# New tables of places for the work order of attention and tail in a hybrid block kernel

## The chip, the cores and the metric

The kernel runs on one core of one Trainium2 chip. The metric is the device time of one launch in microseconds.

## What is computed

The block takes x of shape (2, 1024, 256) in float32 and does four things, each added to x and each behind a layer norm:

- **Attention by a gated delta rule**, 16 heads of 128. Queries, keys and values are projections of the normed x, run through a causal convolution of four taps and a silu. A decay gate per channel and a factor beta per head go with them. For each time step: `S = S * g; delta = (v - k.S) * beta; S = S + k (x) delta; o = q.S`. The output is normed per head, multiplied by a sigmoid gate and projected back with Wo.
- **A feed-forward net** of width 1024 with a silu gate.
- **A selective state space layer** of inner width 512 and 16 states: in-projection, convolution, step sizes by softplus, the scan `h = exp(dt A) h + dt u B; y = h.C + D u`, a silu gate and the out-projection.
- The same feed-forward net again.

## The kernel before

Everything is float32 and x stays in SBUF, transposed. There are two phases, with a barrier of all engines between them (`all_over`).

**Attention** (`att_tensor`, `att_vector`, `att_scalar`, `att_gpsimd`, one function for each engine). Time is cut in 2 segments of 512, so there are 32 turns g of one head and one segment, here called heads; both batches go side by side. A head passes through 13 stages: three convolutions (`conv`, for k, q and v: TensorE projects with L380, ScalarE copies and scales with L937 and L938, VectorE adds three taps with L672, ScalarE takes the silu), `dots` (norms of q and k, L398), `gating` (L414; exponential and logarithm on ScalarE), `turn_v` (transposes, L426), `products` (a mask of decays built by five levels of doubling: TensorE L453, L445 five times, L470; VectorE L749, L756, L758, L767, L768; GpSimd L1172, L1178, L1197, L1199, L1209), `inverse` (a 32 by 32 triangular inverse by doubling, TensorE L482 and, for the last steps, L499 and L507, VectorE L802 and L804, ScalarE L1015), `turn_k` (transposes L519, L529), `solved` (L543, L552), `out_gate` (L570), `state` and `output` (transposes L621, out-projection L630, added to xT by VectorE at L891).

`state` is a chain over the 8 chunks of a head: TensorE predicts (L588, and L593 for the output), VectorE takes the difference (L848), TensorE makes the outer product (L598), VectorE forms the new state (L853), and the next chunk's L588 needs it. At its steps 8 and 17 L604 adds what lies within the chunks.

TensorE's blocks use its array in different shapes: 128*128 for projections and transposes, 128*64 for L588 and L593, 64*128 for L598 and L552, 64*64 for L543 and L604, 128*32 for L398, L445, L453 and L470, and 32*32 for the inverse. The profile writes the shape behind the operation.

Results of most stages pass through three PSUM banks in turn (`take` on TensorE, `turn.next` elsewhere): a block waits until the bank used three takes before has been read.

**The order of work** is not written out. Each stage is a generator on each engine, with the same number of steps (`yield`) on all engines. `braid` merges the generators: every step has a place, a number, and the next step in the program of every engine is the one with the lowest place. In `att_drive` a stage of head g has the places 100 * (g + lag) + at, where `PLACES` holds the lag and the list of a stage. The first FFN unit (one of eight: two nets by four column blocks) is braided into the end of attention by `EARLY_AT`. In the tail, `tail_drive` does the same with scans (64 items a unit, evenly placed), fronts (`FRONT_AT`: everything of the state space layer ahead of its scan, one list for each of four units) and the other seven FFN units (`FFN_AT`).

```
def braid(streams):
    live = [(places[0], n, 0) for n, (steps, places) in enumerate(streams)]
    while live:
        at, n, k = min(live)
        live.remove((at, n, k))
        steps, places = streams[n]
        if next(steps, streams) is not streams:
            live.append((places[min(k + 1, len(places) - 1)], n, k + 1))
```

Each engine works in its own order; semaphores carry the dependencies, and an instruction that waits holds up all that stand behind it on its engine. SP loads each head's weights in a loop of its own during attention (`att_sync`), and in the tail issues the DMAs of `front` and `scan` in the braided order.

**The tail** (`tail_tensor` and the others). FFN units: mean and variance (L1403, L1411), eight blocks of gates (L1423), eight of ups (L1432), two of downs (L1443). Fronts: norms (L1469, L1481), eight projections (L1491, L1502), L1512. Scans: ScalarE takes the exponential (L1908), GpSimd the product with B (L2010), VectorE scans (L1704) and multiplies by C (L1711), and TensorE sums over states (L1521).

Of the kernel before, what the change touches and what calls it, by code (L numbers as in the profile page):

```python
# [35 lines left out]
TILES = NB * T // SEG  # L36
UNITS = NB * NSEG
PLACES = [
    (0, [6.35, 9.83, 30.76, 35.52, 39.59, 39.59]),
    (0, [24.46, 35.88, 43.15, 47.61, 50.78, 50.78]),  # L40
    (0, [40.2, 48.37, 61.83, 62.49, 62.49, 62.49]),
    (0, [66.45, 72.1, 73.85, 105.28]),
    (0, [53.74, 61.7, 62.69, 81.62, 93.61, 103.46, 169.59]),
    (0, [84.02, 121.44]),
    (1, [6.89, 9.65, 15.04, 19.44, 21.1, 23.33, 25.47, 27.36, 32.45, 36.51, 48.5, 56.51, 73.42, 77.42, 80.2]),
    (1, [23.56, 29.24, 29.38, 38.98, 38.98, 45.18, 48.13, 52.96, 52.96, 54.41, 58.87, 60.79, 60.79, 73.73, 74.67,
         75.54, 77.83, 91.54, 91.54, 105.35, 105.35]),
    (1, [89.54, 97.81, 98.47, 104.28]),
    (2, [7.39, 7.39, 9.42]),
    (2, [19.66, 31.86]),  # L50
    (2, [12.55, 14.51, 19.38, 20.74, 21.28, 25.5, 30.47, 36.1, 37.87, 49.21, 54.19, 56.47, 59.02, 62.09, 73.04,
         74.72, 78, 80.17]),
    (2, [33.84, 43.67, 85.96, 91.7, 91.7, 98.17, 98.17, 119.91, 119.91, 121.66, 128.83, 154.28, 173.18]),
]
FRONT_STEPS, FFN_STEPS = 44, 26
FRONT_AT = [
# [12 lines left out]
]  # L69
FFN_AT = [  # L70
# [14 lines left out]
]  # L85
EARLY_AT = [
    [3252.5, 3252.5, 3315.6, 3315.6, 3346.5, 3351.8, 3357.1, 3358.4, 3361.3, 3362.2, 3362.2, 3370.8, 3370.8,
     3375.5, 3387.2, 3387.2, 3393.7, 3418.1, 3418.1, 3420.6, 3424.5, 3424.5, 3605.7, 3626.8, 3664.3, 3664.3],
]
LN_EXP, SILU_TANH = "natural_log_exp_and_others", "silu_and_others"  # L90

# [2082 lines left out]
```

## Time and profile before

| | us |
|---|---|
| three runs | 2701.1, 2700.5, 2714.0 |
| median | 2701.1 |
| the profiled execution | 2704.4 |
| its span, first to last instruction | 2702.6 |
| attention, until the barrier | about 1918 |
| tail | about 785 |

The span is the time on the device between the first and the last instruction; the time of the execution is 1.8 us more. In the rows, PE is TensorE, PEld its weight loads, DVE VectorE, ACT ScalarE and POOL GpSimd; `L445` is line 445 of the kernel; `<-` stands between what is written and what is read. An idle time in brackets names the instruction that ended it.

### The profile page before, as it was taken

How to read it: one execution, taken by the hardware profiler on the slowest of the kernel's cores; microseconds unless marked ns; L12 is line 12 of the kernel's file. 1: busy time of each engine (PE TensorE's matmuls, PEld its weight loads, DVE VectorE, ACT ScalarE, POOL GpSimd, SP SyncE). 2: the span in 40 equal slices, each digit the busy share in tenths (PEclk: the TensorE clock that was granted, in tenths of full speed). 3: DMA queues.
4: the chain of work that ended last, by engine and by line, in shares of the span. 5: the costliest groups of instructions: out<-in, count | busy, mean ns of one | idle time of the engine just before them, and what ended most of it. 6: DMA issues, size and time to landing. Idle time of an engine off the chain costs nothing.

```text
span 2702.6 us, 102733 instructions
## 1 busy us (share of the span) xinstructions
PE 2475.7 (92%) x46512; PEld 1479.0 (55%) x46512; DVE 2133.3 (79%) x3249; ACT 1397.9 (52%) x2649; POOL 1252.6 (46%) x989
## 2 busy tenths in 40 slices
PE   6799999999999999999999999989798899898889
PEld 3466666666666666666666666665343333333333
DVE  3678888888888887888888887883139999999981
ACT  3545555555555565555545555444264646555342
POOL 0555445545554455554555445550025655646540
PEclk8899999999999999999999999998899999999999
DMA  1000000000000000000000000001012433323320
GB/s 54 23 10 13 13 23 13 13 13 23 13 13 13 13 23 13 13 13 23 13 13 13 23 13 13 6 7 51 25 40 94 131 108 116 109 99 122 125 90 16
DMA packets 52070, 105.61 MB, mean 39 GB/s; under 512 B 7085, under 2 KB 11949, under 8 KB 51377
## 3 DMA queue, kind: packets, MB, share of 16 engines
q1 hardware_dynamic: 51632, 99.04, 11.2%
q8 instruction: 365, 5.98, 0.9%
q14 instruction: 73, 0.59, 0.1%
HBM read 96.65 MB, written 2.37 MB: 37 GB/s over the span
## 4 chain that ended last, share of the span: by engine, by line
PE 68%; DVE 19%; issue 7%; ACT 5%; POOL 1%; DMA 0%; SPq 0%; DVEq 0%; ACTq 0%; POOLq 0%
PE bank L380 13%; PE bank L482 6%; DVE hs L1704 6%; DVE cv L672 4%; PE bank L630 4%; PE bank L1521 4%; PE bank L445 3%; PE pair L598 3%; PE pair L1443 3%; PE bank L604 3%; PE pair L588 2%; PE bank L552 2%; PE bank L543 2%; DVE R L758 2%; PE bank L426 2%
## 5 line engine op out<-in xcount | busy, mean ns | idle before, releaser
L672 DVE SCALAR_TENSOR_TENSOR cv<-raw,taps,cv 128x1024 f32<-128x1024 f32 x288 | 403.9, 1412 | 15.1 <-ACT cv L938 13.7
L2010 POOL TENSOR_TENSOR dBu<-dtu,Bn 128x1024 f32<-128x1024 f32 x128 | 306.9, 2399 | 232.6 <-DVE hc L1711 229.5
L380 PE MATMUL bank<-xn,W 128*128 128x512 f32 x768 | 378.8, 617 | 0.0
L1521 PE MATMUL bank<-hc,eye 128*128 128x512 f32 x512 | 252.3, 621 | 54.5 <-DVE hc L1711 54.5
L1908 ACT ACTIVATE bank<-dtv,m_A 128x512 f32<-128x512 f32 x256 | 174.5, 688 | 221.7 <-DVE hs L1704 220.7
L1197 POOL TENSOR_TENSOR kL<-kL,tot 128x512 f32<-128x512 f32 x128 | 204.9, 1601 | 158.9 <-PE bank L445 158.9
L937 ACT ACTIVATE raw<-bank 128x512 f32<-128x512 f32 x192 | 115.8, 603 | 214.6 <-PE bank L380 213.6
L1521 PEld LDWEIGHTS bank<-hc,eye 128*128 128x128 f32 x512 | 94.4, 194 | 198.7 <-DVE hc L1711 104.0
L380 PEld LDWEIGHTS bank<-xn,W 128*128 128x128 f32 x768 | 134.0, 191 | 116.7 <-issue 109.5
L1199 POOL TENSOR_TENSOR R<-R,tot 128x512 f32<-128x512 f32 x128 | 194.7, 1521 | 0.0
L848 DVE TENSOR_TENSOR vT<-vT,pair 128x128 f32<-128x128 f32 x256 | 72.5, 283 | 153.1 <-PE pair L588 151.1
L1711 DVE TENSOR_TENSOR hc<-hs,Cn 128x1024 f32<-128x1024 f32 x128 | 166.8, 1303 | 7.5 <-PE bank L1521 3.1
L1704 DVE TENSOR_TENSOR_SCAN hs<-bank,carry,dBu 128x512 f32<-128x512 f32 x128 | 158.1, 1269 | 4.7 <-ACT bank L1908 4.7
L445 PEld LDWEIGHTS bank<-R,kL 128*32 128x32 f32 x10240 | 114.6, 110 | 81.3 <-DVE Bc L768 34.8
L598 PE MATMUL pair<-vT,kT 64*128 64x128 f32 x1024 | 129.1, 329 | 29.3 <-DVE vT L848 26.1
L1704 DVE TENSOR_TENSOR_SCAN hs<-bank,dBu 128x512 f32<-128x512 f32 x128 | 150.5, 1206 | 3.4 <-ACT bank L1908 2.2
L445 PE MATMUL bank<-R,kL 128*32 128x64 f32 (+1 forms) x10240 | 134.0, 204 | 18.8 <-POOL R L1199 7.2
L630 PE MATMUL bank<-WT,WO 128*128 128x512 f32 x256 | 140.3, 631 | 0.0
L1172 POOL TENSOR_TENSOR R<-qn,gate 128x1024 f32<-128x1024 f32 x32 | 77.7, 2429 | 133.4 <-ACT gate L998 133.4
L598 PEld LDWEIGHTS pair<-vT,kT 64*128 64x128 f32 x1024 | 79.2, 189 | 105.7 <-issue 52.6
L938 ACT ACTIVATE cv<-bank,taps 128x512 f32<-128x512 f32 x192 | 132.9, 692 | 0.0
L1094 ACT ACTIVATE cen<-bank 128x128 f32<-128x128 f32 x256 | 67.4, 278 | 124.7 <-PE bank L604 124.6
(269 smaller groups left out, 5597.3 us busy)
## 6 DMA issues: line engine op xcount, KB each, us to landing
Bn<-ssm_rows SPq DMA_DIRECT2D x128, 256.0 KB, 3.5
Cn<-ssm_rows SPq DMA_DIRECT2D x128, 256.0 KB, 3.1
W<-in_head_w SPq DMA_DIRECT2D x32, 448.0 KB, 3.8
WO<-in_out_w SPq DMA_DIRECT2D x32, 192.0 KB, 2.3
xT<-in_xT SPq DMA_DIRECT2D x1, 2048.0 KB, 8.0
out_xT<-xT SPq DMA_DIRECT2D x4, 512.0 KB, 3.8
xn<-in_w_gate SPq DMA_DIRECT2D x1, 1024.0 KB, 6.8
xn<-in_w_up SPq DMA_DIRECT2D x1, 1024.0 KB, 8.4
```

Of the source, the lines that this page charges most:

```text
L380: m = pe.matmul(psum[bank][:, :], w[:, (kind * KT + k) * P:(kind * KT + k + 1) * P], xn[:, k, b, cols], start=k == 0, stop=k == KT - 1)
L445: m = pe.matmul(o, block(kL[s], c, b, u), r)
L598: m = pe.matmul(psum[CHAIN[b]][:, P:2 * P], kT[s][rows_of(b), c, :], vT[g % 3][rows_of(b), c, :])
L630: pe.matmul(psum[bank][:, :], WO[s][:, (k + 1) * P:(k + 2) * P], WT[s][:, 4 * hh:4 * hh + 4, :].rearrange("p c n -> p (c n)")).then_inc(wo ...
L672: dve.scalar_tensor_tensor(cv[m % 2][:, :, :], raw[m % 2][:, :, i:i + SEG], taps[:, h, KQV[n], i:i + 1], cv[m % 2][:, :, :], MUL, ADD).the ...
L1197: pool.tensor_tensor(Lv[:, :, 0, :], Lv[:, :, 0, :], spread(two[:, :, 1], 2, half), MUL).then_inc(up_l.sem)
L1199: pool.tensor_tensor(Rv[:, 1, :, 1, :], Rv[:, 1, :, 1, :], spread(two[:, :, 0], 2, half), MUL).then_inc(level.sem)
L1521: m = pe.matmul(psum[Y_BANKS[jj]][:, :], eye[:, :], hc[(u * PAIRS + p) % BACK][:, jj, :], start=False, stop=p % HALF_P == HALF_P - 1, skip ...
L1704: dve.tensor_tensor_scan(hs[p % BACK][:, jj, :], psum[A_BANKS[at % NA]][:, :], dBu[p % AHEAD][:, jj, :], carry[:, b, i:i + 1] if seg else ...
L1711: dve.tensor_tensor(hc[p % BACK][:, :, :], hs[p % BACK][:, :, :], spread(Cn[p % DEEP][:, :], 1, DT2), MUL).then_inc(hc_set.sem)
L1908: act.activation(psum[A_BANKS[at % NA]][:, :], dtv[u % 2][:, j, :], ACT.Exp, scale=m_A[:, j, n:n + 1]).then_inc(dA_set.sem)
L2010: pool.tensor_tensor(dBu[at % AHEAD][:, :, :], dtu[s][:, half * DT2:(half + 1) * DT2, :], spread(Bn[at % DEEP][:, :], 1, DT2), MUL).then_i ...
```

## The change

No instruction is added, removed or altered. Other numbers stand in `PLACES` (all 13 lists and three lags), in the four lists of `FRONT_AT` and in the list of `EARLY_AT`. `FFN_AT`, the generators and all waits stay. A list's entries are in the order of the stage's steps; the lists are those of conv (three times), dots, gating, turn_v, products, inverse, turn_k, solved, out_gate, state and output.

```diff
 PLACES = [
-    (0, [6.35, 9.83, 30.76, 35.52, 39.59, 39.59]),
-    (0, [24.46, 35.88, 43.15, 47.61, 50.78, 50.78]),
-    (0, [40.2, 48.37, 61.83, 62.49, 62.49, 62.49]),
-    (0, [66.45, 72.1, 73.85, 105.28]),
-    (0, [53.74, 61.7, 62.69, 81.62, 93.61, 103.46, 169.59]),
-    (0, [84.02, 121.44]),
-    (1, [6.89, 9.65, 15.04, 19.44, 21.1, 23.33, 25.47, 27.36, 32.45, 36.51, 48.5, 56.51, 73.42, 77.42, 80.2]),
-    (1, [23.56, 29.24, 29.38, 38.98, 38.98, 45.18, 48.13, 52.96, 52.96, 54.41, 58.87, 60.79, 60.79, 73.73, 74.67,
-         75.54, 77.83, 91.54, 91.54, 105.35, 105.35]),
-    (1, [89.54, 97.81, 98.47, 104.28]),
-    (2, [7.39, 7.39, 9.42]),
-    (2, [19.66, 31.86]),
-    (2, [12.55, 14.51, 19.38, 20.74, 21.28, 25.5, 30.47, 36.1, 37.87, 49.21, 54.19, 56.47, 59.02, 62.09, 73.04,
-         74.72, 78, 80.17]),
-    (2, [33.84, 43.67, 85.96, 91.7, 91.7, 98.17, 98.17, 119.91, 119.91, 121.66, 128.83, 154.28, 173.18]),
+    (-1, [61.85, 106.12, 122.1, 139.6, 143.3, 146.82]),
+    (0, [21.81, 40.36, 47.08, 47.36, 53.47, 57.55]),
+    (0, [46.86, 50.32, 55.67, 60.17, 65.32, 67.24]),
+    (0, [67.41, 72.3, 76.47, 103.16]),
+    (0, [60.56, 60.56, 63.8, 85.34, 91.54, 94.81, 107.86]),
+    (0, [84.11, 95.7]),
+    (0, [99.66, 99.66, 107.96, 112.78, 118.5, 118.87, 125.56, 130.82, 136.85, 136.85, 148.79, 151.57, 172.94,
+         176.87, 184.71]),
+    (1, [25.31, 33.14, 37.11, 39.91, 40.97, 44.26, 44.94, 50.25, 50.25, 53.23, 53.5, 60.5, 69.14, 77.16, 80.34,
+         82.32, 82.59, 90.86, 90.86, 98.95, 99.79]),
+    (1, [90.68, 91.07, 93.46, 132.71]),
+    (2, [7.01, 7.01, 7.01]),
+    (2, [28.71, 37.38]),
+    (2, [11.53, 13.37, 18.08, 20.17, 22.91, 25.81, 34.31, 37.82, 39.88, 44.95, 48.7, 52.78, 59.34, 63.88, 69.27,
+         76.49, 78.59, 81.97]),
+    (2, [37.83, 42.52, 89.16, 90.28, 90.28, 91.85, 91.85, 110.22, 112.87, 112.87, 116.57, 121.42, 172.93]),
 ]
 FRONT_AT = [
-    [-97.1, -87, -82.1, -52.5, -35, -33.2, -29.1, -24.3, -18.6, -18.6, -16, -10.2, 13.6, 13.6, 13.6, 13.6, 13.6,
+    [-197.6, -140.5, -120.7, -58.3, -54.5, -38.7, -38.7, -22.7, -18.9, -16.9, -3.7, -0.5, -0.5, -0.5, -0.5, -0.5,
...
 ]
 EARLY_AT = [
-    [3252.5, 3252.5, 3315.6, 3315.6, 3346.5, 3351.8, 3357.1, 3358.4, 3361.3, 3362.2, 3362.2, 3370.8, 3370.8,
-     3375.5, 3387.2, 3387.2, 3393.7, 3418.1, 3418.1, 3420.6, 3424.5, 3424.5, 3605.7, 3626.8, 3664.3, 3664.3],
+    [3192.7, 3192.7, 3251.8, 3277.3, 3307.7, 3310.7, 3310.7, 3310.7, 3310.7, 3310.7, 3324.4, 3324.4, 3326.1,
+     3342.2, 3345.1, 3345.1, 3350.8, 3361.7, 3390, 3403.3, 3403.3, 3403.3, 3589.5, 3592.5, 3610.3, 3746.8],
 ]
```

The first steps of conv0 now lie in the head before (lag -1), and `products` has the lag 0 with numbers near 100, which is about where it was. In the other three lists of `FRONT_AT` most numbers move by a few units, none by more than 26.

Written out by `braid`, TensorE's blocks of one head, from the first L588 of one head to the next head's, stand in this order (a number in brackets: chunk or half; g is the head of the state stage):

```
before  588 598 445 588 570 621 621 598 445 588 426 630 380 445 598 630 482 588 570 445 380 598 604 482 380 482
        380 445 588 482 414 598 630 482 588 598 482 414 588 398 598 630 470 482 588 482 598 604 426 519 499 519
        529 529 507 380 453 543 543 552 380
after   588 621 630 598 630 588 445 598 630 380 588 445 598 570 529 482 588 445 570 598 604 482 380 482 588 380
        598 445 482 380 588 482 598 482 414 414 380 588 398 598 630 470 588 482 598 604 482 426 519 499 519 529
        426 507 453 380 543 543 552 445 621
```

## Rows read from the trace of the kernel before

**Rows 1.** The page: busy time by engine, and one DMA issue.

```profile
PE 2475.7 (92%) x46512; PEld 1479.0 (55%) x46512; DVE 2133.3 (79%) x3249; ACT 1397.9 (52%) x2649; POOL 1252.6 (46%) x989
...
W<-in_head_w SPq DMA_DIRECT2D x32, 448.0 KB, 3.8
```

**Rows 2.** Busy time by stage; last: clock, DMA share, GB/s.

```profile
600.00:800.00 200.00, 191.98 (x5258) 130.50 (x5255) 170.74 (x309) 116.62 (x244) 99.61 (x99) 1.00 0.06 17
...
2200.00:2300.00 100.00, 90.13 (x203) 37.22 (x202) 97.80 (x87) 56.70 (x99) 53.58 (x26) 0.98 0.35 114
```

**Rows 3.** The instructions of L1172; a piece of the chain that ended last.

```profile
L1172 POOL TENSOR_TENSOR R<-qn,gate x32: 2350/2366/3400, 78.6 to 1790.7; 128x1024 f32<-128x1024 f32 x32
...
931.45 3.65 PE bank L366 x8
```

**Rows 4.** Busy time of 30 heads, one head, and a later one.

```profile
126.00:1790.70 1664.70, 1580.78 (x41951) 1073.39 (x41949) 1394.52 (x2483) 910.08 (x1895) 852.01 (x762) 0.98 0.05 15
...
681.70:735.50 53.80, 51.57 (x1398) 35.02 (x1397) 46.13 (x84) 30.17 (x64) 27.75 (x28) 1.00 0.05 16
...
1563.90:1621.20 57.30, 54.48 (x1398) 37.24 (x1397) 46.96 (x84) 30.39 (x64) 29.07 (x25) 0.94 0.05 15
```

**Rows 5.** TensorE in order of time: start us, us, what, [idle before].

```profile
689.86 0.49 PE L598 MATMUL pair<-vT,kT 64*128 64x128 f32 x4 [0.17 <-DVE vT L848]
...
694.39 0.49 PE L598 MATMUL pair<-vT,kT 64*128 64x128 f32 x4 [0.45 <-DVE vT L848]
...
695.05 0.76 PE L445 MATMUL bank<-R,kL 128*32 128x32 f32 x64 [0.17 <-DVE Bc L768]
...
719.28 0.49 PE L598 MATMUL pair<-vT,kT 64*128 64x128 f32 x4 [0.17 <-DVE vT L848]
...
727.77 0.44 PE L588 MATMUL pair<-Sx,WT 128*64 128x128 f32 x4 [1.03 <-DVE Sx L853]
...
728.65 0.75 PE L482 MATMUL bank<-Z,XY 32*32 32x32 f32 x64 [0.22 <-ACT Z L1015]
```

**Rows 6.** The same view and head: blocks and what follows them.

```profile
696.83 1.02 PE L630 MATMUL bank<-WT,WO 128*128 128x512 f32 x2
...
697.69 1.88 PE L380 MATMUL bank<-xn,W 128*128 128x512 f32 x4
...
716.71 1.12 PE L630 MATMUL bank<-WT,WO 128*128 128x512 f32 x2
...
717.76 0.75 PE L482 MATMUL bank<-XY,Bc 32*32 32x32 f32 x64
...
730.78 0.66 PE L426 MATMUL bank<-eye,vc 128*128 128x128 f32 x4
...
731.27 0.60 PE L519 MATMUL bank<-eye,R 128*128 128x128 f32 x4
...
731.80 0.69 PE L499 MATMUL bank<-XY,Bo 32*32 32x32 f32 x32
```

**Rows 7.** The same view: three engines at the first two levels.

```profile
684.13 3.69 POOL L1178 TENSOR_TENSOR bm<-masks,bs 128x1536 f32<-128x1536 f32 x1
...
687.12 1.98 PE L380 MATMUL bank<-xn,W 128*128 128x512 f32 x4
...
690.28 1.10 PE L445 MATMUL bank<-R,kL 128*32 128x64 f32 x64
...
692.13 2.00 DVE L758 TENSOR_TENSOR R<-R,gate 128x512 f32<-128x512 f32 x1
...
695.90 1.80 POOL L1197 TENSOR_TENSOR kL<-kL,tot 128x512 f32<-128x512 f32 x1 [1.29 <-PE bank L445]
...
697.67 1.29 POOL L1199 TENSOR_TENSOR R<-R,tot 128x512 f32<-128x512 f32 x1
```

**Rows 8.** The end of attention, on TensorE and ScalarE.

```profile
1838.08 3.68 PE L543 MATMUL bank<-vT,Y 64*64 64x128 f32 x32 [3.25 <-issue]
...
1834.22 1.28 ACT L1103 ACT_TABLE_LOAD   x1
```

22 rows, old and new, of the table FRONT_AT are left out of this document.

## Prediction

> **What bounds the kernel now.** I read the page first. TensorE is busy 92% of the span, VectorE 79% [rows 1]. A change of order makes no work; it can gain only where somebody waits, so the next view is the busy time by stage. In 600 to 800 us, inside attention, TensorE is busy 191.98 of 200 us and VectorE 170.74; at 2200 to 2300, in the tail's scans, VectorE is busy 97.8 of 100 and TensorE 90.1 [rows 2]. So attention is bound by TensorE, with at most 4% idle, and the scans by VectorE, with 2% idle. The heads follow one another: the product of queries and gate (L1172, one a head) runs 32 times from 78.6 to 1790.7, so 31 intervals of 55.2 us [rows 3]. One head at full clock takes 53.8 us, with TensorE busy 51.57; one with a granted clock of 0.94 on average takes 57.3 and 54.48 [rows 4].
>
> TensorE's own list of the head of 53.8 us then says what its 2.2 idle us are: 0.17, 0.45, 0.17, 0.17, 1.03 and 0.22, that is 2.21 [rows 5]. Five of the six wait for VectorE; four of these are in the state chain (prediction, L588; correction on VectorE, L848; outer product, L598; new state, L853), where the table puts two links next to each other or VectorE has older work in front.
>
> **Changes of array shape.** Read from start to start, an L630 block takes 0.86 us where the next block has its shape 128*128 (696.83 to 697.69), and 1.05 where it has not (716.71 to 717.76): a change costs 0.20. After a block of transposes it costs 0.04: 731.27 to 731.80 is 0.53, against 0.49 for the turn before it (730.78 to 731.27) [rows 6]. I wrote out both orders of one head from the tables (stage, head, step; 61 blocks of TensorE). Before, 53 of the 61 successions change shape; after, 52. The count hardly moves, but the kind does: wide 128*128 blocks with a neighbour of their own shape behind them are 1 before (output 9 to conv1 0) and 3 after (output 11 to conv1 0, gating 0 to gating 1, gating 1 to the next head's conv0 0). That is 2 x 0.20 = 0.4 us a head. The rest are transposes, worth 0.04 to 0.1, and cancel.
>
> What speaks against this is the Trainium skill, TensorEngine Tiling (Array Packing), section Key Properties: changing the tiling mode drains TensorE, so the count would matter. By that rule one drain less at 0.20 saves 6 us in the whole kernel, where the rows by kind give 12. The trace agrees that there is a drain, but not that each costs the same (0.20 against 0.04).
>
> **The waits, place by place.** I walk the new order with the start-to-start times of the old one. Zero is the start of the first level (L445).
> - First level. TensorE now runs L445 1.03, a turn of output (L621) 0.53, L588 and L593 0.59, another turn 0.49, L630 1.06: 3.7 us before the outer product L598. VectorE does this level's two products before the correction; in the old trace its L758 ends 3.85 us after the start of L445 (690.28 to 694.13) [rows 7], and L848 some 0.3. So L598 starts at 4.1: 0.4 idle, where it was 0.17 and the link was adjacent.
> - Next state. Behind the correction VectorE has L767, L768 (0.33 each), one addition to xT (0.6) and L853 (0.6), to 5.95; TensorE has L598 0.42 and L630 1.06, to 5.6: 0.35 idle, for 0.45 and 0.17 before.
> - Steps 3 to 9 have 0.7 us or more of other blocks in every gap; nothing waits there, but the third level follows the second by about 4.5 us and the fourth by 3.9, and GpSimd needs 3.9 for the one (0.85, 1.80, 1.29) [rows 7]. I put 0.25 on that.
> - Inverse step 11 has only L598 before it; ScalarE's copy needs about 1.25 us after the L482 start: 0.15 idle.
> - State 11 to 12 was adjacent (0.17); now an L482 is between. State 14 to 15 waited 1.03 for VectorE, which had three convolution products and the cut between; in the new order one of the three is ahead of state 12 and one ahead of state 13, and L853 ends some 0.4 us before it is wanted. Both gaps go.
> - L552 now follows L380 and two L543 directly and wants banks that ScalarE must have read: 0.1.
>
> Sum 1.25, say 1.3 idle in place of 2.2. With the shape changes a head is 0.9 + 0.4 = 1.3 us shorter, 52.5; over 31 heads 40 us. The bounds: if all waits but 0.5 go, 2.1 x 31 = 65; if all waits stay, 0.4 x 31 = 12; the walk is nearer the middle, as two of its six gaps vanish whole and the others are replaced.
>
> **Half clock.** The head of 57.3 us has the same work. All 30 heads from 126.0 to 1790.7 take 1664.7 us, 51 more than 30 x 53.8, at a mean clock of 0.98 [rows 3, 4]; 7 of these are the two extra projections at the middle of attention (the first takes 3.65) [rows 3], the other 44 go mostly with stretches at the lower level, 1.2 GHz. I keep the 44: the new order has two wide blocks side by side ahead of the small dots (L398) and no 1.03 wait behind them, yet no row prices that.
>
> **The end of attention.** Before the last head's L543 at 1838.08 TensorE is idle for 3.25 us, while ScalarE has a table load of 1.28 on its way at L1103 and another right behind it at L1105 [rows 8]; shorter waits for the last head's WT and state follow. EARLY_AT puts the first FFN's norm ahead of them (its step 3 loads the table they want) and five gate projections in front of L588. I take 7 of these, between 0 and 12 (no loss, since these FFN products run there in either order).
>
> **The tail.** The first front's mean goes ahead of eight FFN projections, into TensorE's idle time behind ScalarE; but its norm and input projections stand behind the same sixteen blocks as before, so the first scan starts when it did: 0, between -3 and +3. In the scans VectorE is full; reshuffled fronts move its 2.2 idle us in 100 [rows 2]: 0, plus or minus 8. No queue is moved into: in attention SP runs a loop outside the tables, and a head's weights, which conv0 now wants 45 hundredths of a head sooner, land 3.8 us after an issue that waits for the head before [rows 1]; in the tail the rows of B and C keep their places in the scan, four ahead, and hide there. On GpSimd the halo of conv0 moves with it, past the last level's mask product (L1209), which has the rest of the head as cover.
>
> **Sum.** The profiled execution took 2704.4 us (span 2702.6), 3.3 over the median of 2701.1. 2704.4 - 40 - 7 = **2657 us**.
>
> **Rivals.**
> - GpSimd late at the first level (slower). The first level's VectorE and GpSimd products follow GpSimd's mask product L1178 (3.69 us, done at 687.8, 3.7 before they start at 691.5) [rows 7]. The new order takes L380, L588, L593 and L598 out from between L552 and L445, 3.2 us (687.12 to 690.28), and puts the factors that L1178 waits for (L694) behind two VectorE products, L734 and L739, 1.5 more. So the margin turns into about -1.0, partly hidden, as VectorE is late there anyway. If that chain holds the first level 1.3 us longer than I walked, a head's gain is gone; with 2.4, each head is 1.1 longer: 2704 + 34 - 7 = 2731. For it: the engines hinder each other, as two GpSimd products of one size take 1.80 and 1.29, the longer beside a VectorE product [rows 7]. Against: VectorE's products, not GpSimd's, came last there, and they can start once L1178 is done, 1 us late at most. The Trainium skill, SBUF, section "two separate sides", says that a VectorE operation with two SBUF inputs and a GpSimd one lock each other out for a whole instruction. By that rule L1178 would hold the first product until it ends; the trace agrees in kind (1.80 and 1.29).
> - Waits come back elsewhere: in the heads and at the end; only the 12 us of shape changes stay, 2692, no change.
> - Half clock goes with the 1.03 wait: 44 less, 2613. Or it falls in every head at 57.3 - 53.8 = 3.5: 30 x 3.5 = 105 in place of 44, 2718.
>
> **Chances.** Forecast 0.60; half clock gone 0.12; waits back 0.13; half clock everywhere 0.05; GpSimd late 0.10. Half a per cent (13.5 us) is about what a measurement tells from nothing. Faster 0.72 (first two), same 0.13, slower 0.15. The range 2611 to 2695 takes in the first three cases and both ends of the waits' bounds.
>
> **What would show it.** Intervals of the gate product near 52.5 at full clock; L588 behind state 14 without a wait; L598 and the next L588 near the first level with 0.3 to 0.5 each; L414 to L414 0.86 from start to start; no table load at L1103 in the last head. It is wrong if a wait for GpSimd's R or for bm appears at L445 or L598, if the mean clock falls below 0.96, or if VectorE's idle time in the scans passes 5 us in 100.

## The result and the profile after

The changed kernel took **2620.3 us** (median of 4 runs, 2616.7 to 2621.6), the kernel before beside it on the same chip 2701.4 (2700.5 to 2714.0): a ratio of **0.9694, with a 95% interval of 0.9668 to 0.972**, 3.1% faster. Forecast were 2657 and a range of 2611 to 2695.

The profiled execution took 2619.8 us where that of before took 2704.4; the spans are 2618.0 and 2702.6, 84.6 apart. The gate product of each head (now L1173; every line of the changed kernel is one further down) dates the stages. Its own row answers to [rows 3], and the busy time by stage to [rows 2, 4]. The row of the gate product (times of one in ns, least, median and most, then the first and last start):

```profile
L1173 POOL TENSOR_TENSOR R<-qn,gate x32: 2343/2353/3395, 81.0 to 1711.7; 128x1024 f32<-128x1024 f32 x32
```

Then the windows: 200 us inside attention, 100 in the scans, the 30 heads, one head at full clock (busy time of TensorE, its weight loads, VectorE, ScalarE and GpSimd; the end of a row as in [rows 2]):

```profile
600.00:800.00 200.00, 195.12 (x5301) 134.96 (x5300) 176.37 (x318) 116.22 (x244) 112.72 (x103) 1.00 0.06 17
2120.00:2220.00 100.00, 87.27 (x193) 35.20 (x192) 95.56 (x85) 58.26 (x98) 52.90 (x27) 0.97 0.35 111
126.10:1711.70 1585.60, 1548.50 (x41810) 1061.41 (x41796) 1382.78 (x2484) 921.04 (x1892) 875.80 (x762) 1.00 0.05 15
1083.90:1135.10 51.20, 51.06 (x1397) 35.03 (x1396) 45.92 (x84) 30.59 (x64) 28.99 (x24) 1.00 0.06 17
```

Where the 84.6 us went, stage by stage:

| | before | after | |
|---|---|---|---|
| first gate product | 78.6 | 81.0 | +2.4 |
| 31 intervals to the last one | 1712.1 | 1630.7 | -81.4 |
| from there to the barrier | 125.2 | 120.1 | -5.1 |
| barrier to the first scan | 111.2 | 110.4 | -0.8 |
| scans | 593.5 | 593.9 | +0.4 |
| after the last scan | 82.0 | 81.9 | -0.1 |

So the heads made it. In the 30 heads TensorE's busy time fell from 1580.8 to 1548.5 (32 us) and its idle time, the rest of the stretch, from 83.9 to 37.1 (47 us). The full-clock head went from 53.8 with 2.2 idle [rows 4] to 51.2 with 0.14.

Who TensorE waited for says what the 47 are. In the 30 heads before (us in total, times, longest):

```profile
PE pair L598 <- DVE vT L848: 24.5, 88, 0.9
PE pair L588 <- DVE Sx L853: 22.6, 27, 1.3
PE bank L398 <- issue: 8.2, 13, 1.5
PE bank L482 <- issue: 6.6, 8, 1.5
```

and in those of the changed kernel:

```profile
PE bank L483 <- issue: 13.2, 10, 1.8
PE pair L599 <- DVE vT L849: 5.2, 11, 2.1
PE bank L454 <- issue: 3.7, 8, 0.6
PE pair L589 <- DVE Sx L854: 3.5, 12, 0.7
```

The waits for VectorE in the chain of state are all but gone; what is left is mostly "issue", time in which TensorE waits for no other engine. Over all 31 intervals issue was 24.6 us before and is 21.7 now (idle times of over 0.15 us).

**The first level.** TensorE's own list there (answers to [rows 5, 7]) has no idle time at all:

```profile
1093.19 1.10 PE L446 MATMUL bank<-R,kL 128*32 128x64 f32 x64
1094.22 0.66 PE L622 MATMUL bank<-eye,cen 128*128 128x128 f32 x4
1094.80 0.44 PE L589 MATMUL pair<-S,WT 128*64 128x128 f32 x4
...
1095.88 1.02 PE L631 MATMUL bank<-WT,WO 128*128 128x512 f32 x2
1096.84 0.49 PE L599 MATMUL pair<-vT,kT 64*128 64x128 f32 x4
...
1098.32 0.44 PE L589 MATMUL pair<-Sx,WT 128*64 128x128 f32 x4
```

VectorE's list shows why. Before, it stood still for 4 us ahead of the first correction and then had the level's products behind it:

```profile
689.52 0.29 DVE L848 TENSOR_TENSOR vT<-vT,pair 128x128 f32<-128x128 f32 x1 [4.00 <-PE pair L588]
```

Now the products (L750, L757, L759) lie in that hole, and the last takes 0.70 us where it took 2.00 [rows 7]:

```profile
1089.11 2.18 DVE L735 TENSOR_TENSOR R<-kL,gate 128x1024 f32<-128x1024 f32 x1
...
1091.62 0.68 DVE L750 TENSOR_TENSOR tot<-gate 128x512 f32<-128x512 f32 x1
1094.35 1.14 DVE L757 TENSOR_TENSOR kL<-kL,gate 128x512 f32<-128x512 f32 x1 [2.05 <-PE bank L446]
1095.41 0.70 DVE L759 TENSOR_TENSOR R<-R,gate 128x512 f32<-128x512 f32 x1
1096.04 0.28 DVE L849 TENSOR_TENSOR vT<-vT,pair 128x128 f32<-128x128 f32 x1
```

**The links of the chain.** The starts of the head's eight corrections (L848, now L849), read in one head at full clock of each kernel, are 4.5, 2.4, 6.4, 11.8, 4.3, 3.6 and 5.8 us apart before, and 3.0, 4.8, 4.0, 6.6, 6.1, 6.3 and 4.5 after. Before, one link of 11.8 us stood beside a last stretch of three links (13.6 us) in which VectorE idled 1.0 us in all, and there L588 waited 1.03 [rows 5].

### The profile page after: what moved, and what is told of

It is laid out like the page before. It is cut to its first block, busy times and chain, and to the rows that moved or that the text cites. A ratio compares the mean times of both kernels' runs of the same rounds, so it can differ in the third digit from the quotient of the medians.

```text
span 2618.0 us, 102732 instructions
## 1 busy us (share of the span) xinstructions
PE 2441.7 (93%) x46512; PEld 1462.9 (56%) x46512; DVE 2122.1 (81%) x3249; ACT 1408.8 (54%) x2647; POOL 1273.1 (49%) x989
## 4 chain that ended last, share of the span: by engine, by line
PE 77%; DVE 11%; issue 6%; ACT 4%; POOL 1%; DMA 0%; SPq 0%; DVEq 0%; ACTq 0%
PE bank L381 13%; PE bank L483 7%; DVE hs L1705 6%; PE bank L446 5%; PE bank L631 4%; PE bank L1522 4%; PE pair L599 4%; PE pair L589 3%; PE bank L571 3%; PE bank L605 2%; PE bank L544 2%; PE bank L553 2%; PE bank L415 2%; PE pair L1444 2%; PE bank L594 2%
## 5 line engine op out<-in xcount | busy, mean ns | idle before, releaser
L381 PE MATMUL bank<-xn,W 128*128 128x512 f32 x768 | 378.3, 616 | 0.0
L1198 POOL TENSOR_TENSOR kL<-kL,tot 128x512 f32<-128x512 f32 x128 | 199.8, 1561 | 163.3 <-PE bank L446 162.2
L381 PEld LDWEIGHTS bank<-xn,W 128*128 128x128 f32 x768 | 137.4, 192 | 135.1 <-issue 131.2
L1712 DVE TENSOR_TENSOR hc<-hs,Cn 128x1024 f32<-128x1024 f32 x128 | 172.8, 1350 | 7.9 <-PE bank L1522 3.7
L1200 POOL TENSOR_TENSOR R<-R,tot 128x512 f32<-128x512 f32 x128 | 165.3, 1291 | 0.0
L446 PE MATMUL bank<-R,kL 128*32 128x64 f32 (+1 forms) x10240 | 135.0, 204 | 14.9 <-POOL R L1200 8.0
L446 PEld LDWEIGHTS bank<-R,kL 128*32 128x32 f32 x10240 | 115.3, 111 | 39.9 <-issue 19.7
L1216 POOL TENSOR_TENSOR kL<-kL,tot 128x512 f32<-128x512 f32 x32 | 33.8, 1057 | 211.1 <-PE bank L471 211.1
L599 PE MATMUL pair<-vT,kT 64*128 64x128 f32 x1024 | 126.7, 323 | 6.6 <-DVE vT L849 6.5
L759 DVE TENSOR_TENSOR R<-R,tot 128x512 f32<-128x512 f32 x128 | 107.6, 841 | 26.4 <-PE bank L446 25.2
L1173 POOL TENSOR_TENSOR R<-qn,gate 128x1024 f32<-128x1024 f32 x32 | 77.4, 2418 | 102.2 <-ACT gate L999 102.2
L1179 POOL TENSOR_TENSOR bm<-masks,bs 128x1536 f32<-128x1536 f32 x32 | 101.1, 3160 | 47.6 <-DVE bs L695 47.4
```

The source lines that it names most:

```text
L381: m = pe.matmul(psum[bank][:, :], w[:, (kind * KT + k) * P:(kind * KT + k + 1) * P], xn[:, k, b, cols], start=k == 0, stop=k == KT - 1)
L446: m = pe.matmul(o, block(kL[s], c, b, u), r)
L599: m = pe.matmul(psum[CHAIN[b]][:, P:2 * P], kT[s][rows_of(b), c, :], vT[g % 3][rows_of(b), c, :])
L1198: pool.tensor_tensor(Lv[:, :, 0, :], Lv[:, :, 0, :], spread(two[:, :, 1], 2, half), MUL).then_inc(up_l.sem)
L1712: dve.tensor_tensor(hc[p % BACK][:, :, :], hs[p % BACK][:, :, :], spread(Cn[p % DEEP][:, :], 1, DT2), MUL).then_inc(hc_set.sem)
```

## Experiments

All of them change numbers of `PLACES` or `FRONT_AT`, or the loads that SP issues. "Heads" is the time from the first gate product to the last, 1712.1 before and 1630.7 after.

**Is it the bunch of tap products ahead of the 1.03 us wait? (e1)** The kernel before, conv2's taps spread over three links:

```diff
-    (0, [40.2, 48.37, 61.83, 62.49, 62.49, 62.49]),
+    (0, [40.2, 48.37, 54.3, 59.9, 65.3, 65.3]),
```

> The kernel before with one list altered: the three convolution products of v on VectorE (steps 2 to 4 of conv2) at 54.3, 59.9 and 65.3, as in the changed kernel, in place of 61.83, 62.49, 62.49. TensorE's order is untouched. Theory W (the gain came from TensorE's waits for VectorE): the wait of 1.03 us a head before L588 behind state step 14 goes, 31 x 1.03 = 32 us, to about 2669. Theory H (the stretches at 1.2 GHz hang on that wait): they fall too, from 61 us within the heads to 20 or fewer, and another 20 us go, to about 2649. Theory S (array shapes alone carry the gain): no change, 2701.

Measured: 2710.8 us beside 2701.8, ratio 1.0031 (1.0019 to 1.0043), slower by 0.3%. The wait at L588 went and came back one link earlier, at L598:

```profile
PE pair L598 <- DVE vT L848: 50.2, 88, 1.6
```

The three taps are not the cause by themselves: where they were moved to, VectorE was as full. None of the three expected times came. TensorE's time at the lower level of its clock (1.2 GHz) fell even so, from 75 us in the heads to 48, but idle time put down to issue at L482 rose from 7.1 to 15.8; what was gained at one was lost at the other, and half clock does not hang on the wait at L588 alone.

**Can bunching them undo the gain? (e2)** The changed kernel, with two of the taps moved onto a third:

```diff
-    (0, [46.86, 50.32, 55.67, 60.17, 65.32, 67.24]),
+    (0, [46.86, 50.32, 65.32, 65.32, 65.32, 67.24]),
```

> The changed kernel with the same three products bunched behind state step 13 (places 65.32, 65.32, 65.32). TensorE's order is that of the changed kernel. Theory W: the new state (L854) behind state step 14 is late again by about 1 us a head, 2620 + 31 = 2651. Theory H: the stretches at 1.2 GHz come back with it, 2665 or more. Theory S: 2620.

Measured: 2707.0, ratio to before 1.0022 (1.0009 to 1.0035): the whole gain is gone, more than any of the theories had, as the wait is 2.2 us and not 1. Heads 1708.1. One wait a head does it, and clock:

```profile
PE pair L589 <- DVE Sx L854: 65.8, 31, 3.1
```

TensorE spent 126 us of these heads at the lower level of its clock (1.2 GHz), against 27 in the changed kernel and 75 before. Nearly every head has a half-clock stretch, and it begins within 2 us of the end of that wait of 2.2. The head is 54.7 where the changed one is 51.2 at full clock: 2.2 for the wait and half of the slow stretch of 3.4 us for the clock are 3.9, of which 3.5 show. Issue takes 2.5 us in these heads where it took 21.7: idle time of that kind goes where TensorE stands still anyway.

**Changes of shape alone (e3).** Two of the three wide pairs are split; the changes are 54 a head in place of 52:

```diff
-    (-1, [61.85, 106.12, 122.1, 139.6, 143.3, 146.82]),
+    (-1, [65.4, 106.12, 122.1, 139.6, 143.3, 146.82]),
...
-    (0, [60.56, 60.56, 63.8, 85.34, 91.54, 94.81, 107.86]),
+    (0, [60.45, 60.56, 63.8, 85.34, 91.54, 94.81, 107.86]),
```

> The changed kernel with gating 0 placed before inverse step 11 and the next head's conv0 0 behind state step 13, so that the three wide 128*128 blocks in a row (L415, L415, L381) have other shapes between them: 54 shape changes a head in place of 52, both added ones behind blocks of 512 columns. If such a change costs 0.20 us and TensorE has no idle time to take it up: 2 x 0.20 x 31 = 12 us more, 2632. If a change costs 0.04 as behind transposes: 2622 or 2623. If the VectorE wait decides instead, no change.

Measured: 2628.9, ratio to before 0.9724 (0.97 to 0.9749), 8.6 us over the changed kernel; but its five runs lie between 2613 and 2635, so this is a direction and no price. The profiled heads took 6.0 more, and the best of them 51.3 in place of 51.0: 0.3 a head.

**Waits of ScalarE (e4).** conv2's first projection goes right behind conv1's second one. For that the silu of conv0 moves ahead of it (its last number), and the last level's products move ahead of state step 10, to keep the links apart:

```diff
-    (-1, [61.85, 106.12, 122.1, 139.6, 143.3, 146.82]),
+    (-1, [61.85, 106.12, 122.1, 139.6, 143.3, 143.6]),
...
-    (0, [46.86, 50.32, 55.67, 60.17, 65.32, 67.24]),
+    (0, [44.0, 50.32, 55.67, 60.17, 65.32, 67.24]),
...
-    (0, [99.66, 99.66, 107.96, 112.78, 118.5, 118.87, 125.56, 130.82, 136.85, 136.85, 148.79, 151.57, 172.94,
+    (0, [99.66, 99.66, 107.96, 112.78, 118.5, 118.87, 125.56, 130.82, 136.85, 136.85, 147.5, 151.57, 172.94,
```

> An attempt to go further: in the changed kernel conv2 0 moves directly behind conv1 1 (two L381 blocks side by side, 51 shape changes a head), and the last level's L446 goes between state steps 9 and 10 to keep the chain's distance. By the price of a shape change: 0.20 x 31 = 6 us less, 2614. Rival: ScalarE must take the silu of k before it reads that projection, so its copies for the inverse come late, and each head waits 0.3 us or more: 2625 or above.

Measured: 2684.3, ratio to before 0.994 (0.9927 to 0.9954), 64 us over the changed kernel, with one change of shape fewer a head (51). The waits took it:

```profile
PE bank L483 <- ACT Z L1016: 30.6, 30, 1.0
PE pair L589 <- DVE Sx L854: 19.1, 39, 0.7
```

**What "issue" is (e5, e6, e7).** In the changed kernel's heads the longest idle times put down to issue, 1.0 to 1.8 us, are inside blocks of L483. TensorE's list at one of them:

```profile
337.91 0.59 PE L483 MATMUL bank<-Z,XY 32*32 32x32 f32 x45
340.31 0.37 PE L483 MATMUL bank<-Z,XY 32*32 32x32 f32 x19 [1.82 <-issue]
```

and a window that begins 2 us later (the granted clock, third from the end, is 0.50, the lower level of 1.2 GHz):

```profile
342.40:345.80 3.40, 3.40 (x41) 3.07 (x38) 2.80 (x5) 2.79 (x6) 0.49 (x2) 0.50 0.02 5
```

The DMA view of 335 to 341 us, a head's weights (448 KB and 192 KB) and one transfer on the instruction queue; narrowed down to 337.9 to 339.5, it has the instruction transfer (16 KB) start right there, when the weights are through:

```profile
q1 hardware_dynamic: 288, 0.66, 33.9%
q8 instruction: 1, 0.02, 1.0%
...
W<-in_head_w SPq DMA_DIRECT2D x1, 448.0 KB, 3.7
```

In the heads of both kernels every idle time of over 0.35 us that is put down to issue ends 2.2 to 2.9 us after such a transfer began, and these transfers are some 5 us apart (337 in the 31 intervals of either). That suggests that TensorE had run out of instructions; nothing in the trace says so outright. In the changed kernel's heads there are 24 of them (20.8 us), and at 15 (16.3 us) weights were on their way around that transfer. e5 cuts the weights into pieces, e6 leaves out the loads from the third head on (the later heads compute with the first ones' weights), e7 is e5 on the kernel before:

```diff
-                    sp.dma_start(W[(g + 1) % 2][:, :], a["head_w"][(g + 1) % H]).then_inc(w_loaded[(g + 1) % 2].sem, 16)
+                    for j in range(4):
+                        r = slice(32 * j, 32 * j + 32)
+                        if j:
+                            sp.wait_ge(w_loaded[(g + 1) % 2].sem, 64 * ((g + 1) // 2) + 16 * j)
+                        sp.dma_start(W[(g + 1) % 2][r, :], a["head_w"][(g + 1) % H][r, :]).then_inc(w_loaded[(g + 1) % 2].sem, 16)
...
```

> The changed kernel, but a head's weights come in pieces: W as four transfers of 32 partitions, WO as two of 64, each issued when the one before has landed. Theory F (fetch): TensorE's idle time that the profile puts down to issue is the wait for the next 16 KB of its own instructions; where such a transfer (instruction queue) falls into the 640 KB of weights, it comes late. In the changed kernel's trace every issue gap of over 0.35 us ends 2.2 to 2.9 us after an instruction transfer began, and about 17 of them (18 us, 1.0 to 1.8 us each at L483) have weights on their way at the time; three of these gaps are followed by a stretch at half clock of 3.41 us. With pieces, an instruction transfer has at most 112 KB in front of it: 12 to 20 us less, 2600 to 2608, issue idle under 12. Theory O (order): the gaps belong to the many small blocks in a row, whatever SP does: 2620 within 4, issue idle still 20 to 25. Theory D (the loads last longer, six landings in place of two, and hinder more transfers): 2625 to 2635.

> The changed kernel without the loads of W and WO from the third head on; the later heads compute with the weights of the first ones, so the output is another. Nothing else changes. Theory F: no issue gap with weights on their way is left; 14 to 22 us less, 2598 to 2606, and the half-clock stretches near 342, 397 and 452 us are gone. If the run with pieces lies within 3 us of this one, the pieces take away all that the loads cost. Theory O: 2620 within 4.

> The kernel before with the weights in the same pieces. Its trace has 8 issue gaps (8.5 us) with weights on their way and 13 (11 us) without, most of the latter at L398. Theory F: 5 to 10 us less than the kernel before, 2692 to 2696, so that the ratio of the two orders stays about 0.967 to 0.97 also with pieces: the change's gain is then not in where its instruction transfers fall. Rival: a good part of the change's gain is that; then this run comes nearer than 2685.

Measured, beside a kernel before of 2698.9: e5 2607.5 (ratio 0.9661, 0.9637 to 0.9684), e6 2608.1 (0.9663, 0.964 to 0.9686), e7 2682.2 (0.9941, 0.992 to 0.9962). By these medians the pieces take away all that the loads cost. The waits for issue in the heads, first of e5, then of e6:

```profile
PE bank L454 <- issue: 7.4, 13, 1.0
...
PE bank L483 <- issue: 4.8, 10, 1.0
```

```profile
PE bank L454 <- issue: 5.2, 12, 0.9
...
PE bank L483 <- issue: 3.2, 6, 0.8
```

L483 falls from 13.2 to 4.8 and 3.2, and in both the half-clock stretches at 342, 397 and 452 us are gone. What stays is about 15 us of issue in e5's profile and 11 in e6's, where under 12 was expected of e5; half is at L454 (3.7 in the changed kernel), and e6 shows that it does not need the loads. Its cause is open. e7 gained 17 us, more than the 5 to 10 of the expectation, and lies below the 2685 that was to speak for the rival: issue fell from 24.6 to 13.8 us in its heads and the time at the lower level from 75 to 48. But e5 stands to it as 0.972, where the changed kernel stands to the one before as 0.969. By these two ratios the loads account for about a tenth of the change's gain.

The dots point at the order of the blocks too. The block L398 has 128 small matmuls; in the kernel before it stands behind another small block, a wide one and a state product, in the changed one behind three wide blocks (L415 twice, L381) and a state product. From its start to the next block's it took 1.23 us in the first heads of before, but 1.4 to 3.0 in 15 heads between 396 and 1218 us, 11.2 us above 1.23 in all; in the changed kernel it takes 1.23 in all but one, 0.6 above. Such a block of before, and of after:

```profile
614.36 0.73 PE L398 MATMUL bank<-kL 128*32 128x32 f32 x62
...
615.42 0.63 PE L398 MATMUL bank<-qn 128*32 128x32 f32 x49 [0.17 <-issue]
615.98 0.49 PE L598 MATMUL pair<-vT,kT 64*128 64x128 f32 x4
```

```profile
1122.59 2.16 PE L415 MATMUL bank<-hfa,W 128*128 128x512 f32 x4
1124.59 1.88 PE L381 MATMUL bank<-xn,W 128*128 128x512 f32 x4
1126.40 0.44 PE L589 MATMUL pair<-S,WT 128*64 128x128 f32 x4
...
1126.98 0.73 PE L399 MATMUL bank<-kL 128*32 128x32 f32 x62
...
1128.21 0.49 PE L599 MATMUL pair<-vT,kT 64*128 64x128 f32 x4
```

The other traces bear out that it goes with the order, and not with the loads: the block takes 10 to 12 us above 1.23 in each of the four kernels with TensorE's old order (e7 with its pieces: 10.3), and 0 to 1.1 in the ten with the new one or a variant of it. The row of three wide blocks is not needed for it: e3 splits it, has only one of them, L381, right ahead of L399, and shows 0.6. Which of the other moves did it was not tried.

**The tail's tables (e8).** The changed kernel with the four old lists of `FRONT_AT`:

```diff
-    [-197.6, -140.5, -120.7, -58.3, -54.5, -38.7, -38.7, -22.7, -18.9, -16.9, -3.7, -0.5, -0.5, -0.5, -0.5, -0.5,
+    [-97.1, -87, -82.1, -52.5, -35, -33.2, -29.1, -24.3, -18.6, -18.6, -16, -10.2, 13.6, 13.6, 13.6, 13.6, 13.6,
...
```

> The changed kernel with the old numbers in the four lists of FRONT_AT; attention and EARLY_AT are the new ones. My theory: the tail's tables are worth nothing, 2620 within 4. The rival: the new front's numbers carry part of the 84 us, since from the barrier to the first scan the changed kernel takes 110.4 against 111.2 and after the first scan it is even: 2624 to 2632. The other rival: the new numbers cost something, 2612 to 2616.

Measured: 2625.3, ratio to before 0.9727 (0.9706 to 0.9748); the interval overlaps with that of the changed kernel, though the time itself lies in the rival's 2624 to 2632. The profile decides: there 2.9 of the 3.6 us of span lie in the heads, whose tables are the same, and from the last gate product to the end it is 0.7: 231.9 to the first scan for 230.5, 593.1 of scans for 593.9. The tail's tables are worth about nothing. That heads of one order differ by 3 us between two programs is the scatter of this stage.

**The taps again (e9).** The kernel before, the first tap now behind the correction:

```diff
-    (0, [40.2, 48.37, 61.83, 62.49, 62.49, 62.49]),
+    (0, [40.2, 48.37, 56.6, 59.9, 65.3, 65.3]),
```

> The kernel before with three of the tap products of conv2 spread again, but the first of them (L672) now behind the correction L848 of that state step and the two products of the level, not ahead of them: in the first attempt it stood ahead, and the wait of 1.03 us at L588 came back as 0.90 at L598. VectorE then reaches L853 about 1.3 us later than before, which is about when TensorE comes for it, past L598, L482 and L414. Theory W (what bounds is the chain of state behind VectorE's queue, and a wait costs its length and a share of half clock): L588 waits at most 0.3 us a head in place of 1.03, 20 to 30 us less; of the 14 stretches at half clock in attention 10 follow that wait, and 1.7 us go with each 3.41 of them, 10 to 15 us more: 2655 to 2680. Rival (the place of three products is worth nothing, since the wait comes back at the next link, as it did): 2700 within 5.

Measured: 2734.9 beside 2704.9, ratio 1.0115 (1.0093 to 1.0137). A miss: neither theory had it slower. The wait of 1.03 at L588 shrank (22.6 us in the heads became 7.9), and others came, ahead of it and behind it:

```profile
PE pair L598 <- DVE vT L848: 31.4, 113, 0.9
PE pair L588 <- DVE S L853: 24.9, 30, 1.1
PE bank L482 <- ACT Z L1015: 19.4, 24, 0.8
```

The tap took 1.98 us in its new place, for the 1.28 that I had put in. With e1, two attempts of two to place these taps in the last three links of the old order failed. That the order has to make room elsewhere is argued from them, not shown.

**The hole at the first level (e12).** The changed kernel; only the first level's products go behind the first correction again:

```diff
-    (0, [99.66, 99.66, 107.96, 112.78, 118.5, 118.87, 125.56, 130.82, 136.85, 136.85, 148.79, 151.57, 172.94,
+    (0, [99.66, 99.66, 112.5, 112.78, 118.5, 118.87, 125.56, 130.82, 136.85, 136.85, 148.79, 151.57, 172.94,
```

> The changed kernel with the first level's step of products (L446; VectorE L750, L757, L759) behind the first correction of the chain (L849) again, at 112.5 in place of 107.96. TensorE still has L446, L622 and L631 between L589 and L599. In the kernel before, VectorE stands idle for 3.99 us ahead of this correction in a head at full clock and 7.7 us in the whole head; in the changed one the longest idle time is 2.16 and the sum 5.3, and the gaps between the eight corrections are 3.1 to 6.6 us where they were 2.4 to 11.8. Theory V (part of the gain is that the level's products fill this hole): VectorE has 0.3 + 2.5 of products, 0.85 of L768 and L769 and 0.7 of L854 to do, 4.65 us behind the first L589, where TensorE has 4.15 of blocks: 0.5 us a head at the second L589, 16 us in all, and with some half clock up to 30: 2635 to 2650. The hole ahead of L849 is back at 3 us or more. Rival 1 (the spacing of the later links alone counts): 2620 within 5, though the hole is back. Rival 2 (the whole of the 84 us hangs on it): over 2670.

Measured: 2691.2 beside 2698.2, ratio 0.9969 (0.9955 to 0.9982): 71 of the 81 us between the two kernels are lost by one number, as rival 2 had it (over 2670). In the profile 63 us of that are in the heads and 7 between the last gate product and the barrier. VectorE in such a head, in order of time, and GpSimd's part of the same list:

```profile
851.40 0.29 DVE L849 TENSOR_TENSOR vT<-vT,pair 128x128 f32<-128x128 f32 x1 [3.22 <-PE pair L589]
851.61 0.68 DVE L750 TENSOR_TENSOR tot<-gate 128x512 f32<-128x512 f32 x1
...
853.28 1.99 DVE L759 TENSOR_TENSOR R<-R,gate 128x512 f32<-128x512 f32 x1
...
855.86 0.67 DVE L892 TENSOR_TENSOR xT<-xT,bank 128x512 f32<-128x512 f32 x1
856.45 0.59 DVE L854 SCALAR_TENSOR_TENSOR Sx<-S,tot_chunk,pair 128x128 f32<-128x128 f32 x2
```

```profile
852.72 2.00 POOL L1200 TENSOR_TENSOR R<-R,gate 128x512 f32<-128x512 f32 x1 [1.37 <-PE bank L446]
```

The hole is back (3.22), and L759 is back at 1.99: it starts behind GpSimd's L1200, where in the changed kernel it starts 0.12 us ahead of it (1095.41 and 1095.53) and is through in 0.70. L854 ends 5.6 us after the correction began. The terms of my 4.65 add up to 4.35 only, and they lacked above all 1.1 at the products (3.6 in place of 2.5, as L759 takes 1.99) and the 0.6 of L892. The other loss I had not seen: with L446 gone from between L553 and L589, that L589 waits for ScalarE's WT. TensorE's waits in the heads:

```profile
PE pair L589 <- DVE Sx L854: 49.2, 31, 3.1
PE pair L589 <- ACT WT L1058: 18.5, 30, 1.2
```

TensorE's busy time in a full-clock head is 51.03, as in the changed kernel, and the head lasts 53.3 for 51.2: the difference is these two waits. The gain is no sum of parts: this one number takes back 71 us and the two of e2 take back 87, so no share of the 81 belongs to either alone.

**Pieces beside the whole loads (e10, e11).** e10 is the changed kernel unedited, e11 is e5 once more.

> The changed kernel as it is, beside the next run on one chip: 2614 to 2624, ratio to before 0.968 to 0.971.

> The changed kernel with the weights in pieces, a second time, beside the changed kernel on one chip: by theory F 8 to 16 us less than it; 2602 to 2612.

Measured on one chip, before 2704.9: e10 2620.7 (2613.0 to 2621.9, ratio 0.9687, 0.9662 to 0.9712), e11 2608.9 (2603.0 to 2614.8, ratio 0.965, 0.9624 to 0.9676). The pieces are worth 12 us there, 0.45%; e5, on another chip than the changed kernel's first runs, was 13 us under them, 9 by its ratio. The intervals of the ratios overlap, so the sign rests on the two medians and on the issue waits that go.

## Why the prediction was right, and where its sizes were off

The forecast had the sign, the place and the mechanism; it was 37 us short of the gain.

- **Shape changes, 12 us: about so.** From the start of the two L415 over L381 to L589 it is 3.63 us in 27 of 29 heads (3.81 in the one shown above), where before two lone L414 at 1.056 and an L380 at 1.914 make 4.03: 0.40 a head for two new pairs, as forecast. e3, which splits two pairs, gave 0.3 back. The rule of the Trainium skill (TensorEngine Tiling (Array Packing), Key Properties) would have made it 6 us for one change fewer. e4, with 51 changes, was 64 us slower: the count decides nothing here, where waits cost more.
- **Waits, 28 us of the 40: mis-sized, and the largest miss.** I walked the new order to 1.3 us idle a head; in the full-clock heads it is 0.14. The step that failed is the first level. I had VectorE's products end 3.85 us after the start of L446, with L758 at its old 2.00. They end 2.9 after it (1093.19 to 1096.11): L750 runs before the level starts (1091.62), which the walk had left in line, and L759 takes 0.70, as it now starts just ahead of GpSimd's L1200. So 0.4 and 0.35 of the walk are 0. The 0.25 for the third and fourth level, the 0.15 at the inverse and the 0.1 at L552 show no row either. What I counted as gone did go. That is 2.1 a head in place of 0.9, more than my upper bound had (2.1 with the shapes, 65 us, for 0.5 of idle time left): 2.1 + 0.4 = 2.5, against 53.8 - 51.2 = 2.6 measured; 31 of these are 81, though that this is the gain of the heads to the microsecond is luck (next point).
- **Half clock, kept at 44 us: half of it went, and the 44 stayed by luck.** The time at the lower level in the heads fell from 75 to 27 us, worth about 24, as half of it is lost. Where it went follows the waits: 9 of the 13 stretches before come within 3.1 us behind the wait at L588 (once with an issue gap of 0.96 between), in the changed kernel's heads one of six follows a wait for the chain, at 138 us; three follow an issue gap of 1.0 to 1.8. Yet the 30 heads last 49.6 us more than 30 at full clock, as before (50.7): their busy time beyond that of the full-clock head fell from 34 to 17 us, their idle time beyond it rose from 17 to 33. The sum was right there with a wrong content; what the half clock gave back was lost in idle time outside the full-clock heads. The rival "half clock goes with the 1.03 wait" (2613, 0.12) was a part of the truth, and it was wrong to hold the two apart as cases: e2 shows one bringing the other, and e1 that half clock comes behind other idle times too.
- **GpSimd late at the first level (slower): did not come.** R and bm hold nothing up; the only such waits (L446 for R, 13.7 us) are in the first heads, before 100 us, as in the kernel before (12.0). The mechanism that I leaned on is there, though in another place. L735 takes 2.18 beside GpSimd's L1173 (which runs from 1087.85 on for 2.35) where it took 1.21, and L757 1.14 beside L1179. By the Trainium skill (SBUF, section "two separate sides") the one locks the other out for an instruction; the trace agrees, 1.21 against 2.18, 0.70 against 2.00. It falls where VectorE has its hole, so it costs nothing. e12 puts it back on the path.
- **The end of attention, -7: -5.1.** No table load stands in the last head ahead of L544, and its idle time is 0.91 for 3.25 [rows 8]; L500 waits 1.43 for VectorE and 1.32 for issue in its stead. `EARLY_AT` was not run by itself.
- **The tail, 0: -0.5** by the table, and e8. VectorE idles about 4 us in 100 in the scans, the scans last as long.
- **What remains of the sum.** -81.4 in the heads are 49.6 of TensorE's idle time (100.5 before, 50.9 after) and 31.8 of its busy time. Most of the idle time is waits for other engines, 76.9 before and 27.5 after. For the busy time 24 of half clock, 12 of shapes and 3 or so of the slow dots that the profile counts as busy make 39, so some 7 us were lost elsewhere. Four of them are one pair of neighbours that got dearer: L599 before L483 takes 0.55 from start to start, where L598 before L482 took 0.42, once a head. The rest was not traced.

## What to carry to other kernels

Where a chain runs between two engines and one of them has a long hole in a round, fill the hole first: in the old order moving work inside the full stretch only moved the wait (e1, e9), and one step put back out of the hole cost 71 of 81 us (e12). That does not make the bunch harmless: in the new order bunching the taps cost 87 (e2). Price a wait on TensorE at its length and at the half clock that may follow; in e2 that was 2.2 and 1.7 us a head. Idle time called "issue" is worth a look at the instruction queue: splitting big loads that ran beside a stream of small matmuls gave 12 to 17 us (e7, e11).

## What the hardware showed that was not expected

- TensorE seems to run dry of instructions: issue gaps of up to 1.8 us within a block, each of over 0.35 us ending 2.2 to 2.9 us after a 16 KB transfer on the instruction queue began; with 640 KB of weights ahead of that transfer, 13.2 us of them at L483, without 3.2 (e6). The Trainium skill, Runtime: NRT & Kernel Launch, section Instruction fetch mechanics, says that crossing a boundary between 16 KiB blocks of instructions is mostly hidden. If the gaps are that, about 21 us of a kernel of 2620 were not hidden here. How much the order of small blocks alone costs was only read (L398, 1.23 to 3.0 us), not tried by itself.
- With one wait of 2.2 us in nearly each head, most heads had one stretch at half clock (e2, 126 us in all), while the heads of the changed kernel with 0.14 us of idle time had none.
